# Graph-attention kernel: adjacency codes transposed by DMA on SyncE's queue instead of by TensorE

## The reference

```python
e = leaky(einsum('bid,bjd->bij', x * a0[:, 0], x))          # layer 0, slope 0.2
alpha = sigmoid(where(adj == 1, e, -max))                    # codes 2 to 4 use a1 to a3
x = layernorm(x + einsum('bij,bjd->bid', alpha, x) + bias)
Hh = x @ W                                                   # layer 1
s, d = Hh @ a_src, Hh @ a_dst
e = where(adj != 0, exp(-leaky(s[:, None] + d[None, :])), 0)
x = layernorm(x + elu((e @ Hh) / rowsum(e)))
```

## Time and profile before

| | us |
|---|---|
| median of 3 runs (lowest, highest) | 1443.07 (1442.54, 1446.59) |
| the profiled execution | 1447.32 |
| its span in the trace | 1445.6 |
| PE busy | 1346.6 (93%) |
| DVE busy | 1063.0 (74%) |
| ACT busy | 935.2 (65%) |
| POOL busy | 854.3 (59%) |

### The profile page before, as it was taken

One profiled execution on the slowest core, in us unless ns is written; L12 is line 12 of the kernel. 1 busy time (PEld: TensorE's weight loads), 2 busy tenths in 40 slices (PEclk: granted clock), 3 DMA queues, 4 the chain that ended last, 5 costly groups with the idle time before them and its releaser, 6 DMA issues.

```text
span 1445.6 us, 29637 instructions
## 1 busy us (share of the span) xinstructions
PE 1346.6 (93%) x8898; PEld 1206.4 (83%) x8898; DVE 1063.0 (74%) x2654; ACT 935.2 (65%) x2197; POOL 854.3 (59%) x1228
## 2 busy tenths in 40 slices
PE   4799999999999999999999999999999999999986
PEld 3688888988889888888988889888988888888875
DVE  3487877777777777877777777787877787777754
ACT  3676757667585666757657685676757657575742
POOL 3464847558384664837557394764838557384732
PEclk9799999999999999999999999999999999999988
DMA  4113031221303213131321303222121322303100
GB/s 105 30 30 74 23 50 60 45 64 29 76 18 51 65 30 75 22 50 54 51 58 32 73 18 51 65 37 68 25 47 54 51 62 33 69 18 51 37 1 31
DMA packets 55185, 68.18 MB, mean 47 GB/s; under 512 B 5488, under 2 KB 38640, under 8 KB 55152
## 3 DMA queue, kind: packets, MB, share of 16 engines
q0 software_dynamic: 18432, 33.56, 14.8%
q1 hardware_dynamic: 36720, 34.22, 7.3%
HBM read 84.55 MB, written 16.78 MB: 70 GB/s over the span
## 4 chain that ended last, share of the span: by engine, by line
PE 52%; POOL 20%; DVE 11%; issue 7%; DMA 5%; ACT 3%; DVEq 1%; POOLq 0%; SPq 0%; ACTq 0%
PE acc_bank L1203 17%; POOL coef_lo L346 9%; PE hh_bank L1182 5%; DMA code_nat<-in_adj 4%; PE acc_bank L1089 4%; PE acc_bank L1090 4%; PE acc_bank L1091 4%; PE lg_bank L1089 4%; PE lg_bank L1091 4%; PE lg_bank L1090 4%; DVE coef L865 3%; POOL rstd L367 3%; PE tr_bank L1124 3%; POOL rstd L357 2%; POOL var_eps L354 2%
## 5 line engine op out<-in xcount | busy, mean ns | idle before, releaser
L1203 PE MATMUL acc_bank<-H,coef 128*128 128x258 f32 x2048 | 472.9, 384 | 8.9 <-ACT reluP L589 8.1
L1203 PEld LDWEIGHTS acc_bank<-H,coef 128*128 128x128 f32 x2048 | 383.6, 191 | 64.5 <-issue 10.6
L346 POOL TENSOR_TENSOR coef_lo<-coef,coef_hi 128x1024 fp32r<-128x1024 f32 x128 | 306.0, 2391 | 75.1 <-ACT coef_hi L538 73.4
L1089 PE MATMUL acc_bank<-h_hi,coef_hi 128*128 128x256 f32 x1024 | 300.2, 293 | 0.0
L1090 PE MATMUL acc_bank<-h_lo,coef_hi 128*128 128x256 f32 x1024 | 289.0, 282 | 0.0
L1091 PE MATMUL acc_bank<-h_hi,coef_lo 128*128 128x256 f32 x1024 | 288.6, 282 | 0.0
L865 DVE SCALAR_TENSOR_TENSOR coef<-G,E_col,codeT 128x256 f32<-128x256 f32 x512 | 229.3, 513 | 43.0 <-PE acc_bank L1203 36.8
L1089 PEld LDWEIGHTS acc_bank<-h_hi,coef_hi 128*128 128x128 f32 x1024 | 197.3, 193 | 1.1 <-issue 0.2
L1090 PEld LDWEIGHTS acc_bank<-h_lo,coef_hi 128*128 128x128 f32 x1024 | 197.6, 193 | 0.0
L1091 PEld LDWEIGHTS acc_bank<-h_hi,coef_lo 128*128 128x128 f32 x1024 | 197.3, 193 | 0.0
L332 POOL DMA_DIRECT2D code_nat<-in_adj x128 | 73.5, 575 | 202.1 <-PE tr_bank L1124 181.5
(11 more groups left out here) (80 smaller groups left out, 2613.3 us busy)
## 6 DMA issues: line engine op xcount, KB each, us to landing
code_nat<-in_adj POOLq DMA_DIRECT2D x128, 256.0 KB, 3.6
x_raw<-in_x SPq DMA_DIRECT2D x16, 1024.0 KB, 5.6
out<-x SPq DMA_DIRECT2D x128, 128.0 KB, 1.7
W_ext<-in_L_gnn_W SPq DMA_DIRECT2D x1, 256.0 KB, 2.8
score<-in_L_gnn_a SPq DMA_DIRECT2D x1, 256.0 KB, 6.0
bias_bc<-in_L_gnn_bias SPq DMA_DIRECT2D x1, 128.0 KB, 3.9
a_col<-in_L_gnn_a SPq DMA_DIRECT2D x4, 1.0 KB, 2.1
```

The lines of the kernel that those rows point to most:

```text
L346: nc.gpsimd.tensor_tensor(coef_lo[:, t % 4, :, :], blocks(coef[:, t % 4, :]), f32(coef_hi[:, t % 4, :, :]), ALU.subtract).then_inc(S.lo0, 1)
L1089: nc.tensor.matmul(dst, lhs_hi, rhs_hi, start=first, stop=False)
L1203: ins = nc.tensor.matmul(acc_bank[t % 2][:, 0:HC], coef[:, SLOT1[t], J * P:(J + 1) * P], H[:, J, :], start=J == 0, stop=J == NT - 1)
```

## The change

The 64 PE transposes of codes and the 8 copies on ACT and DVE are gone for each graph. SP issues one DMA transpose for each block, from `code_nat` to `codeT`, 8 for each graph, on the queue that also carries the loads of `x` and the stores of the output. `turn_codes(b + 1, t)` waits for the block's load and for the last uses of the old `codeT` block. In `graph(b)` all eight stand ahead of the eight stores and the load of x. All who waited for a PE transpose or for a copy now wait for the completion of the DMA transpose (`codes_turned`), POOL's loads among them.

```diff
+            def turn_codes(b, t, first):
+                sp.wait_ge(F.adj_loaded[t % 4], 32 * b + 16 * (t // 4) + 16)
+                sp.sem_inc(sp_past, 1)
+                if not first:
+                    for made in (F.mask1, F.codes_watched):
+                        sp.wait_ge(made, NT * (b - 1) + t + 1)
+                        sp.sem_inc(sp_past, 1)
+                sp.dma_start_transpose(codeT[:, t, :].rearrange("p (j i) -> p j i", i=P),
+                                       code_nat[:, t % 4, :]).then_inc(F.codes_turned[t % 4], 16)
-            def graph(b, loads):
+            def graph(b, loads, nxt=True):
+                if nxt:
+                    for t in range(NT):
+                        turn_codes(b + 1, t, False)
                 for t in range(NT):
...
             load_x(F, 1)
+            for t in range(NT):
+                turn_codes(0, t, True)
...
-                    pool.wait_ge(S.codes, NT * b + t - 3)
+                    if S is F:
+                        pool.wait_ge(F.codes_turned[t % 4], 32 * b + 16 * (t // 4))
...
             def watch_codes(b, t):
-                act.wait_ge(F.codes_kept, NT * b + t + 1)
+                act.wait_ge(F.codes_turned[t % 4], 32 * b + 16 * (t // 4) + 16)
...
                 dve.wait_ge(F.tanh, NT * b + t + 1)
-                dve.wait_ge(F.codes_kept, NT * b + t + 1)
-
+                dve.wait_ge(F.codes_turned[t % 4], 32 * b + 16 * (t // 4) + 16)
...
-            def next_codes(b, t):
-
-                pe.wait_ge(F.codes_kept, NT * (b + 1) + t - 1)
-                transpose_codes(F, b + 1, t)
```

More of the change, by code:

```diff
@@ L57, in __init__ @@
         self.tanh = sem(tag + "tanh")
-        self.codes = sem(tag + "codes")
-        self.codes_kept = sem(tag + "codes_kept")
+        if general:
+            self.codes = sem(tag + "codes")
+        if general:
+            self.codes_kept = sem(tag + "codes_kept")
+        else:
+            self.codes_turned = [sem(tag + f"codes_turned{i}") for i in range(4)]
         self.mask0 = sem(tag + "mask0")
@@ L123, in two_graph_layers @@
     XT_STEP = {2: 0, 3: 1, 4: 2, 5: 3}
-    ACT_CODES = 4
     EDGE = NT // 2
@@ L298, in _ @@
             graph(LAST - 1, False)
-            graph(LAST, False)
+            graph(LAST, False, False)
             for s in F.out_stored:
@@ L329, in load_adj @@
                 if not first:
-                    pool.wait_ge(S.codes, NT * b + t - 3)
+                    if S is F:
+                        pool.wait_ge(F.codes_turned[t % 4], 32 * b + 16 * (t // 4))
+                    else:
+                        pool.wait_ge(S.codes, NT * b + t - 3)
                 pool.dma_start(code_nat[:, t % 4, :], adj_v[b, t, :, :]).then_inc(S.adj_loaded[t % 4], 16)
@@ L507, in tanh_row, with keep_codes @@
                                      scale=0.5).then_inc(F.tanh, 1)
-            def keep_codes(S, b, t, prev):
+            def keep_codes(S, b, t):
                 act.wait_ge(S.codes, NT * b + t + 1)
-                if prev:
-                    act.wait_ge(S.mask1, NT * b + t + 1 - NT)
-                    act.wait_ge(S.codes_watched, NT * b + t + 1 - NT)
                 nc.scalar.activation(codeT[:, t, :], tr_bank[t % 2][:, :].bitcast(BF16),
@@ L629, in graph @@
                     scale_scores(b + 1, 6)
-                    keep_codes(F, b + 1, 0, True)
                 last_G(F, b, False)
@@ L633, in graph @@
                     scale_scores(b + 1, 7)
-                    keep_codes(F, b + 1, 1, True)
                     high_x(F, b + 1, 0)
                     high_x(F, b + 1, 1)
-                    keep_codes(F, b + 1, 2, True)
                 for t in range(NT + 1):
@@ L649, in graph @@
                     if nxt:
-                        if t + 3 < ACT_CODES:
-                            keep_codes(F, b + 1, t + 3, True)
                         if t == 0:
@@ L665, in _ @@
                 scale_row(0, J)
-            for t in range(NT):
-                keep_codes(F, 0, t, False)
             for J in range(NT):
@@ L686, in _ @@
                     for t in range(NT):
-                        keep_codes(GEN, b, t, False)
+                        keep_codes(GEN, b, t)
                         for k in range(KINDS):
@@ L968, in graph @@
                         mask0_rest(b + 1, t + 3 - NT)
-                    if nxt and ACT_CODES <= t + 3 < NT:
-                        keep_codes(b + 1, t + 3)
                     if t >= 1:
@@ L1131, in mirror @@
                         continue
-                    if m >= 2:
+                    if m >= 2 or not isinstance(b, int) or b > 0:
                         pe.wait_ge(F.mirror_used, NM * b + m - 1)
-                    else:
-                        pe.wait_ge(F.codes_kept, NT * b + NT - 1 + m)
                     pe.wait_ge(F.tanh, NT * b + t + 1)
@@ L1259, in graph @@
                     scores_chunk(b + 1, 5)
-                    for t in range(2):
-                        pe.wait_ge(F.mirror_used, NM * b + NM - 1 + t)
-                        transpose_codes(F, b + 1, t)
                 spread_last(F, b)
@@ L1271, in graph @@
                         mirror(b + 1, t + 3 - NT)
-                    if nxt and t in (3, 4):
-                        next_codes(b, t + 3)
                     aggregate1(F, b, t)
[L1275 to L1278, removed]
                     if nxt and t == 0:
@@ L1294, in _ @@
                 scores(0, J)
[L1295 to L1298, removed]
             for t in range(4):
```

## The result

The changed kernel takes 1463.63 us (median of 4 runs, 1462.95 to 1467.24) against 1443.76 us before (median of 4): a ratio of 1.0134, 95% interval 1.0114 to 1.0154. It is 1.3% slower, where 1378 us and faster were forecast.

What follows compares the result with a forecast made beforehand. PE, busy for 93% of the span, was taken as the bound. From the profiled 1447.3 us, 58 (PE's stream) and 10.5 (start) gave 1379, or 1374.6 against the median; 3 added for POOL: 1378 us, range 1366 to 1540, likeliest case 1366 to 1392.

Steps and rivals of the forecast that it cites:

- Time off PE's stream: Stage change to the next graph: transposes gone, relu earlier, load wait gone; 3.85 us per graph, 58 us over 15.
- the forecast place: Start of aggregate1(3) in the stage change: claimed to move from 732.69 to about 730.1 us.
- The start: Graph 0 on ACT: without copies of codes, tanh can follow the scores at 42.7, not 53.20; 10.5 us off.
- T = 3.6 us: SP's queue: spacing at which DMA transposes finish one behind another; taken as 3.6 us, range 1.7 to 11.8 us.
- The guess of 1024 pieces: DMA engines: a transpose moving rows of 256 bytes has 1024 pieces at 46 ns each, 2.9 us on 16 engines.
- Who waits for T: POOL's load of block 6, low_x and power1 behind block 2's transpose: free of charge up to T = 4.3.
- just fits: POOL reaches power1(b, 0) at 728.9, its input coming at about 729, so T = 3.6 costs nothing.
- a slow transpose: Rival: POOL, then the whole loop, waits for slow DMA transposes; slower from T = 5.8, 1543 us at T = 8; chance 0.31.
- the formula: POOL's chain: a graph is late by 3 x (T - 3.6) - 2 us, if that is positive.

Runs made afterwards that it cites:

- number 3: Kernel before, with low_x computing only 8 of 256 columns in all graphs but the first: 1434.64 us, 0.9933 of before.
- number 5: Changed kernel with the four low_x moved ahead of POOL's three loads of codes: 1379.71 us, 0.9546 of before.
- number 1: Kernel before, with POOL's low_x made to wait until aggregate1(1) is done; no DMA transpose: 1504.59 us, 1.0407 of before.
- number 2: Changed kernel with low_x computing only 8 of 256 columns in all graphs but the first: 1381.56 us, 0.9568 of before.
- number 4: Changed kernel with 54 extra PE transposes of the identity per graph, filling PE's waits after aggregate1(2): 1442.51 us, 0.9988 of before.
- number 9: Changed kernel with low_x ahead of the loads and each DMA transpose issued twice, one after the other has landed: 1511.85 us, 1.0454 of before.
- number 7: Changed kernel with six slots for raw codes instead of four and semaphores for each block, POOL's order unchanged: 1390.14 us, 0.9603 of before.
- number 8: Changed kernel with low_x ahead of the loads and ACT's last two h_hi ahead of block 0's relu: 1397.09 us, 0.9661 of before.

## Why the prediction was wrong

- **Time off PE's stream, 3.85 us for a graph:** right in mechanism, too large in size. With `low_x` out of the way in both kernels it was 2.8 us (number 3). In number 5 `aggregate1(3)` starts at the forecast place, and a period is 82.9 us (748.66 to 831.54) against 86.6 us, 3.7 us less, but there two errors cancel. The late masks begin 1.2 us earlier than before and not 1.8 us (PE now waits for DVE's scores ahead of `aggregate1(0)`, which starts at 718.61 - 3.79 = 714.82 instead of 715.11, 0.3 us earlier where the forecast had 0.9). Against that, they take 3.26 us instead of 4.03 us, as `low_x` no longer meets them, a gain of 0.8 us that no term had. The changed kernel itself got none of it.
- **The start, 10.5 us:** right; tanh starts 10.7 us earlier.
- **T = 3.6 us:** right as the median time to landing (3.0 to 11.4 us). As a spacing it was smaller: SP issues a transpose in 1.23 us without waiting for the one before, and POOL's three loads were released at 720.48, 722.27 and 725.59, so 1.8 and 3.3 us apart. Block 2 was turned by 725.59 - 3.79 = 721.8, where 723.4 was forecast. In all, POOL's loads waited 210.8 us for the transposes, against 181.5 us for PE's before. The guess of 1024 pieces was good too: 171888 - 36720 = 135168 packets more on the queue, 1056 for each transpose. They took 21.3% of 1461.9 us less 7.3% of 1445.6 us on 16 engines, 24 ns each, and not 46. The figure of the Trainium skill, VectorE: DVE Perf Modes (The three transpose paths), 1309 ns for a block by DMA, doesn't add up over eight blocks here: one transpose of eight landed in 3.6 us and not in 10.5 us. The Trainium skill, Advanced Engine Details and Errata (X-Bar Transpose), says "TRN2 transpose DMAs are as fast as regular DMAs". The trace agrees in the time to landing (3.6 us, and 3.7 us for the 256 KB adjacency block), but not in the load on the DMA engines. The plain transfers of that queue before moved 34.22 MB in 7.3% of the span, 324 GB/s of busy time; the transposes, by the difference of the two runs, moved 33.57 MB at 163 GB/s.
- **Who waits for T: this step failed.** The prediction read POOL's chain only forwards, to `power1(b, 0)`, and found that the later `low_x` "just fits". That it did: `power1` still waited 5.53 us for DVE. By the forecast's own times, `low_x` would run from 723.4 + 0.53 = 723.9 to 728.9, and the masks of blocks 6 and 7 from 724.38 - 1.8 = 722.6 to 726.6. It thus had the two meet for 2.7 us, and put no term for that into the sum. It took the 4.97 us of `low_x` and the 4.03 us of the masks as durations that stay when the two are moved against each other. `low_x` came 726.14 - 3.79 - 720.38 = 2.0 us later and the masks 724.38 - (726.93 - 3.79) = 1.2 us earlier, and the meeting grew from 1.0 to 4.2 us. Numbers 1 and 2 show from both sides that this decides: put into the kernel before it costs 61 us, and taken out of the changed one it gives 82 us. The 1382 us of number 2 lie near the forecast 1378 us, again in part by luck: the kernel before gains 10 us by the same cut, so the transposes themselves are worth 53 us and not 68.
- **The sign was in the rows.** The late eight masks took 4.03 us, and the eight before them, which that section of rows doesn't have, 3.25 us.

```profile
715.60 3.25 DVE L865 SCALAR_TENSOR_TENSOR coef<-G,E_col,codeT 128x256 f32<-128x256 f32 x8
```

The same instructions have two prices, 0.8 us apart, and `low_x` ends 0.97 us after the slower ones begin. The Trainium skill, SBUF — State Buffer (SBUF: two separate sides), states the rule: DVE and GpSimd have a pair of ports in common, held by one of them for a whole instruction, and a DVE instruction with two inputs in SBUF needs it against a GpSimd instruction that reads SBUF. The trace agrees with it in kind, in number 1 at 7.43 us for 3.25 us of masks. It goes further, as one DVE instruction was held over four POOL instructions in a row. I hadn't weighed it.
- **What followed:** behind PE's wait of 2.64 us the granted clock fell to 0.50, and with the waits filled it stayed at 1.00, which gave 21 us back (number 4). No term of the forecast had the clock.
- **The rivals:** slower was one of them, but as a slow transpose. The change was slower with a fast one. Its price was too low: with 5.2 us for a block the formula takes 3 x (5.2 - 3.6) - 2 = 2.8 us for a graph, and number 9, without `low_x` in the way, lost 132 / 15 = 8.8 us against number 5. How much of that is the doubled traffic stays open.

## What to carry to other kernels

When a change moves work on POOL, look at what DVE does at the new time, not only at who waits for POOL. Compare the same DVE instruction in two places: where it is longer than its minimum, look for POOL beside it, and price the whole overlap. And when work leaves the bounding engine, its neighbours' order may need to be set again: the change alone lost 1.3%, with four instructions moved it gained 4.5%, and those four moved alone lost 5.7%.

## What was not expected of the hardware

- One DVE instruction of 0.48 us was held for 5.5 us, while four POOL instructions of 1.24 us ran one behind another: DVE didn't get in between them. There (first change of stage, masks from 108.78, `low_x` from 110.69) DVE had been under way for 1.9 us when POOL began, and POOL's 4.93 us were not lengthened. In number 7 the same pair of instruction kinds met with DVE's eight under way first by 1.45 us, and POOL paid (6.66 us instead of 4.97 us) while DVE's 3.25 us stayed. In number 8 DVE was under way first too, by 0.45 us, and paid 4 us all the same. What decides who waits stays open.
- While transposes and loads of codes were in flight together, the DMA engines' busy share reached 1.02 for 10 us (718.6 to 728.4) at only 153 GB/s. By estimate from the packets, a transposed block of 256 KB costs the 16 engines 24 ns x 1056 / 16 = 1.6 us.
